# Attention prologue: x loaded first, the stacks cleared in halves, and their row blocks moved to partitions 0-23 and 64-87

## What is computed

```python
q, k, v = split(x @ wq + bq), split(c @ wk + bk), split(c @ wv + bv)
scores = einsum("bhqd,bhkd->bhqk", q, k) * scale
o = einsum("bhqk,bhkd->bhqd", softmax(scores), v)
x + merge(o) @ wo + bo
```

## Time and profile before

| | |
|---|---|
| runs | 5312.48 us median of 3 (5310.64 to 5335.13) |
| profiled execution | 5331.78 us |
| its span, first to last instruction | 5330.1 us |
| X: SP's first load, first scores | 2517.45, 2568.38 us |
| F: the same | 3087.01, 3145.86 us |
| N: the same | 4058.88, 4105.02 us |
| Y: the same | 4643.76, 4689.13 us |

### The profile page before, as it was taken

The page is one execution under the profiler, slowest core; times in us unless marked ns, Lnnn a source line. Parts: engine busy times, 40 slices in busy tenths (PEclk is TensorE's granted clock), DMA queues, the critical chain, the costliest instruction groups (busy, mean ns, idle before and its releaser), DMA issues. The chain is left out here.

```text
span 5330.1 us, 104454 instructions
## 1 busy us (share of the span) xinstructions
PE 4007.7 (75%) x29689; PEld 2312.2 (43%) x29692; DVE 4292.2 (81%) x8421; ACT 2778.3 (52%) x6469; POOL 3235.8 (61%) x3458
## 2 busy tenths in 40 slices
PE   5887888778788887785789958886292888779953
PEld 2333333333333333332466635665282666556632
DVE  5999999999999999996688867775145788767778
ACT  4555555555555555553577724444373455444535
POOL 6888878888888887885677733333544222333345
PEclk8999898998998998988899969996695899889975
DMA  2101111111011111110566546665115555466621
GB/s 85 68 34 70 70 70 38 68 70 70 38 66 70 70 56 50 70 68 14 95 107 111 88 81 111 108 114 157 50 53 118 100 105 105 74 120 113 116 57 32
DMA packets 320191, 420.69 MB, mean 79 GB/s; under 512 B 40000, under 2 KB 301712, under 8 KB 309136
## 3 DMA queue, kind: packets, MB, share of 16 engines
q1 hardware_dynamic: 315536, 408.35, 33.1%
q0 software_dynamic: 4352, 8.95, 0.5%
HBM read 307.65 MB, written 109.58 MB: 78 GB/s over the span
## 5 line engine op out<-in xcount | busy, mean ns | idle before, releaser
L2205 POOL TENSOR_TENSOR m_h<-m_dtu,m_Bb 128x512 f32<-128x512 f32 x1024 | 1595.7, 1588 | 152.6 <-PE bank L1838 150.1
L1838 PE MATMUL bank<-m_h,ident 128*128 128x512 f32 x2048 | 1237.7, 695 | 411.4 <-DVE m_h L2104 405.0
L1838 PEld LDWEIGHTS bank<-m_h,ident 128*128 128x128 f32 x2048 | 368.4, 209 | 1088.9 <-DVE m_h L2104 937.1
L2098 DVE TENSOR_TENSOR_SCAN m_h<-m_dA,m_h 128x512 f32<-128x512 f32 x512 | 773.5, 1511 | 0.5
L2104 DVE TENSOR_TENSOR m_h<-m_h,bank 128x512 f32<-128x512 f32 x1024 | 673.1, 657 | 12.7 <-PE bank L1831 12.7
L2098 DVE TENSOR_TENSOR_SCAN m_h<-bank,m_h 128x512 f32<-128x512 f32 x512 | 620.8, 1212 | 16.7 <-ACT bank L1986 9.5
L1986 ACT ACTIVATE m_dA<-m_dt,m_A 128x512 f32<-128x512 f32 x512 | 366.9, 717 | 356.5 <-DVE m_h L2098 350.1
L1986 ACT ACTIVATE bank<-m_dt,m_A 128x512 f32<-128x512 f32 x512 | 352.5, 688 | 379.3 <-DVE m_h L2098 273.7
L691 DVE TENSOR_REDUCE x_nm<-bank 128x4 f32<-128x308 f32 x512 | 242.4, 474 | 166.6 <-PE bank L364 163.7
L535 ACT ACTIVATE x_sm<-bank,x_nm 128x77 f32<-128x77 f32 x1024 | 318.2, 336 | 62.2 <-DVE x_nm L691 61.8
L691 DVE TENSOR_REDUCE f_nm<-bank 128x4 f32<-128x512 f32 x256 | 175.9, 688 | 111.6 <-PE bank L364 110.9
(11 more groups left out here) (424 smaller groups left out, 10364.4 us busy)
## 6 DMA issues: line engine op xcount, KB each, us to landing
m_Bb<-m_B SPq DMA_DIRECT2D x32, 4096.0 KB, 12.1
x_Ks<-x_k_parts SPq DMA_DIRECT2D x32, 462.0 KB
x_q_parts<-x_qp SPq DMA_DIRECT2D x32, 384.0 KB, 4.2
x_Qs<-x_q_parts SPq DMA_DIRECT2D x32, 384.0 KB
f_Ks<-f_k_parts SPq DMA_DIRECT2D x16, 768.0 KB
a_Ks<-a_k_parts SPq DMA_DIRECT2D x16, 768.0 KB
x_xp<-x_stage SPq DMA_DIRECT2D x32, 256.0 KB
x_Qs<-x_q_parts SPq DMA_DIRECT2D x32, 256.0 KB
```

The lines of the kernel that those rows point to most:

```text
L1838: pe.matmul(banks[4 + c], ident[:], h[:, k % RING, :], start=(s == 0), stop=(s == NS - 1)).then_inc(s_ya.sem, 1)
L2098: v.tensor_tensor_scan(h[:, k % RING, :], decays[k % AHEAD], h[:, k % RING, :], 0.0, ALU.mult, ALU.add).then_inc(s_h.sem, 1)
L2205: pool.tensor_tensor(h[:, k % RING, :], dtu[:, d, c, :], Bb[:, d, s, :], ALU.mult).then_inc(s_dB.sem, 1)
```

## The change

SP loads x of the first group before the weights, and in F the weights of the LayerNorm ahead of the others. The waits for all weights move: on TensorE and ScalarE behind the turning and copying of the first x, on VectorE in front of the first group's values (in F of its norm), on GpSimd they are gone. Each stack is cleared in halves, one per group: Ks by VectorE at its start and behind the first group's preparation, Qs by ScalarE in the same places, as an `activation` that copies a constant times 0 over a half as fp32. nmT and pT are cleared by VectorE behind the first group's preparation. The second halves have a semaphore of their own, on which SP waits before the second group's fill. The six blocks move from partitions 0-47 to 0-23 and 64-87 (Q: 24 rows at 0, 16 at 64, 8 at 80), and Ks is filled by two transfers of 24 rows.

```diff
-    PARTS, ROWS = 3, 6 * DH
+    PARTS = 3
     K_TIMES = (3, 2, 1)
+    Q_ROWS = (0, 8 * DH, 10 * DH)
+    K_ROWS = ((0, 0, 3), (8 * DH, 3, 6))
+    FILLS = len(Q_ROWS) + len(K_ROWS)
...
+        zeros = half_pow[:, 0:1].unsqueeze(1).to_broadcast([P, H, GT // 2])
...
             def fill_stack(g, par):
+                if isinstance(g, int) and g == 1:
+                    sp.wait_ge(s_zero1.sem, 2)
...
-                at = 0
-                for parts in K_TIMES:
-                    fill(Qs[at * DH:(at + parts) * DH, par], dram_q[par, 0:parts])
-                    at += parts
-                fill(Ks[0:ROWS, par], dram_k[par])
+                for row, parts in zip(Q_ROWS, K_TIMES):
+                    fill(Qs[row:row + parts * DH, par], dram_q[par, 0:parts])
+                for row, lo, hi in K_ROWS:
+                    fill(Ks[row:row + (hi - lo) * DH, par], dram_k[par, lo:hi])
...
             load_x(0, 0)
+            load_weights()
             load_x(1, 1)
...
         def _(pe):
-            pe.wait_ge(s_w.sem, 16 * NW)
...
                     if g == 0 or slot[u] < 0:
                         prep(u, g, g)
+                    if g == 0 and u == "x":
+                        pe.wait_ge(s_w.sem, 16 * NW)
...
-            act.wait_ge(s_w.sem, 16 * NW)
-            if rms or bq is not None:
+            def clear_queries(par, zeroed):
+                act.activation(Qs[:, par].bitcast(F32), zeros, ACT.Copy, scale=0.0).then_inc(zeroed, 1)
...
+            clear_queries(0, s_zero.sem)
             for g in range(2):
                 for u in uses:
...
                     if u != "v" and (g == 0 or slot[u] < 0):
                         prep(u, g, g)
+                    if g == 0 and u == "x":
+                        scale_bias()
+                if g == 0:
+                    clear_queries(1, s_zero1.sem)
...
-            dve.memset(Ks[:], 0.0).then_inc(s_zero.sem, 1)
-            if gate is None:
-                dve.memset(nmT[:], 0.0).then_inc(s_zero.sem, 1)
-            if sk < P:
-                dve.memset(pT[:], 0.0).then_inc(s_zero.sem, 1)
-            dve.wait_ge(s_w.sem, 16 * NW)
-            dve.wait_ge(s_setup.sem, 1)
+            dve.memset(Ks[:, 0], 0.0).then_inc(s_zero.sem, 1)
...
                         if g == 0 or z < 0:
+                            if g == 0 and f is (front_norm if ln is not None else value_rows):
+                                v.wait_ge(s_w.sem, 16 * NW)
                             f(v, ch, g, g)
+                    if g == 0:
+                        if gate is None:
+                            v.memset(nmT[:], 0.0).then_inc(s_zero.sem, 1)
+                        if sk < P:
+                            v.memset(pT[:], 0.0).then_inc(s_zero.sem, 1)
+                        v.memset(Ks[:, 1], 0.0).then_inc(s_zero1.sem, 1)
...
         def _(pool):
-            pool.wait_ge(s_w.sem, 16 * NW)
-            pool.sem_inc(s_step, 1)
...
-            pool.memset(Qs[:], 0.0).then_inc(s_zero.sem, 1)
```

More of the change, by code:

```diff
@@ L166, in attention @@
         lvar = sb("lvar", [P, 2, GB]) if ln is not None else None
-        s_w = sem("weights"); s_setup = sem("setup"); s_zero = sem("zeroed"); s_xp = sem("x_loaded"); s_xr = [sem(f"residual_loaded{l}", 16) for l in range(2)]
+        s_w = sem("weights"); s_setup = sem("setup"); s_zero = sem("zeroed"); s_zero1 = sem("second_stacks_zeroed"); s_xp = sem("x_loaded"); s_xr = [sem(f"residual_loaded{l}", 16) for l in range(2)]
         s_xpfree = sem("x_used"); s_pb = sem("proj_written", NU); s_pf = sem("proj_evacuated", NU)
@@ L171, in attention @@
         s_mid = sem("mid_ready", 2); s_lo = sem("lo_ready", 2)
-        s_ps = sem("parts_stored", 16 * (PARTS + 1)); s_stk = [sem(f"stack_loaded{l}", 16 * (PARTS + 1)) for l in range(2)]
+        s_ps = sem("parts_stored", 16 * (PARTS + 1)); s_stk = [sem(f"stack_loaded{l}", 16 * FILLS) for l in range(2)]
         s_ln = sem("front_var", 1); s_lp = sem("front_pow", 1); s_xn = sem("front_norm", 1)
@@ L210, in _, with load_weights @@
         def _(sp):
-            n = 0
             def load_w(dst, src):
                 sp.dma_start(dst, src).then_inc(s_w.sem, 16)
[L214 to L228, removed]
+            def load_weights():
+                if ln is not None:
+                    for j, t in enumerate(ln):
+                        load_w(lnw[:, j, :], t.rearrange("(a d) -> a d", a=1).to_broadcast([P, D]))
+                for j, t in enumerate((wq, wk, wv, wo)):
+                    load_w(w[:, j, :], t)
+                for j, t in enumerate((bq, bk)):
+                    if t is not None:
+                        load_w(bqk[:, j:j + 1], t.rearrange("(d a) -> d a", a=1))
+                if rms:
+                    for j, t in enumerate(rms):
+                        load_w(bqk[:, j:j + 1], t)
+                if bv is not None:
+                    load_w(bvb[:], bv.rearrange("(a d) -> a d", a=1).to_broadcast([P, D]))
+                if bo is not None:
+                    load_w(bob[:], bo.rearrange("(a d) -> a d", a=1).to_broadcast([P, D]))
             def load_x(g, par):
@@ L480, in _, with scale_bias @@
         def _(act):
-            act.wait_ge(s_w.sem, 16 * NW)
-            if rms or bq is not None:
-                act.activation(bqk[:, 0:1], bqk[:, 0:1], ACT.Copy, scale=scale).then_inc(s_bq.sem, 1)
-                act.wait_ge(s_bq.sem, 1)
+            def clear_queries(par, zeroed):
+                act.activation(Qs[:, par].bitcast(F32), zeros, ACT.Copy, scale=0.0).then_inc(zeroed, 1)
+            def scale_bias():
+                act.wait_ge(s_w.sem, 16 * NW)
+                if rms or bq is not None:
+                    act.activation(bqk[:, 0:1], bqk[:, 0:1], ACT.Copy, scale=scale).then_inc(s_bq.sem, 1)
+                    act.wait_ge(s_bq.sem, 1)
             def evac(g, u, dst, src, **k):
@@ L576, in _ @@
                     if rms and u == "qn":
+                        if g == 0:
+                            act.wait_ge(s_setup.sem, 1)
                         root(g)
```

## The result

The changed kernel takes 5272.1 us (median of 5 runs, 5259.4 to 5279.7) against 5322.9 us for the kernel before on the same chip (5 runs, 5310.6 to 5335.1): a ratio of 0.9902, 95% interval 0.9885 to 0.9919. It is 1% faster, inside the range and of the sign forecast. 43 us were forecast, 51 came. That the forecast in us (5269) lies nearer than that is luck: the three runs it started from were low, 5312.5, where the five sessions of this study have medians of 5319.0 to 5327.4 for the kernel before.

The account below looks back on a forecast made before the run. TensorE's idle time before the first scores of four attention stages, mainly behind GpSimd's clearing, was the target: 11.4 + 15.9 + 1.6 + 10.4 + 4 = 43 us off the 5312.48 us median gave 5269 us, range 5237 to 5300.

Parts of the forecast that it names:

- X, F, Y: Prologues of gated cross attention, attention with LayerNorm in front, plain cross attention: 11.4, 15.9 and 10.4 us won.
- The mechanism of the clearing: In X, GpSimd's 13.75 us clearing of Qs holds VectorE's first q cast at 9.79 us instead of 0.43.
- N: Prologue of the attention with RMS norms: x copied out earlier, after ScalarE's clearing, 1.6 us won (0.5 to 2.8).
- The fill: Stack fills before the first scores, in the new partition layout: 1 us less each, 4 us over four stages.
- My count of rows per engine (8 against 7): Fills: the busiest DMA engines carry 8 rows instead of 7, 1.7 us more per fill at the same pace.
- Rival (a): Fills run at the first microsecond's pace: 12 us more come off, 55 in all, 5257 us; chance 0.14.
- (b): Fills get longer by 2.5 us, also delaying Y's loop: 20 us won, 5292 us; chance 0.11 with its like.
- (c): K's two transfers on twelve engines bound Y's loop: at 6 us longer fills 47 us lost, 5359; chance 0.06.
- "Groups in the loops as long as before": Attention loops after the prologues: a sign of being right was that their groups take as long as before.
- Rival (d): Prologues: the clearing was not what held VectorE, so only about 14 us is won, 5298 us; chance 0.03.

Follow-up runs that it names:

- e5: Kernel before, with GpSimd's clearing of the Q stacks cut into 32 instructions instead of one; ratio to before 1.0001.
- e2: Changed kernel with the six blocks back in partitions 0-47 and K filled by two transfers of 24 rows; ratio to before 0.9957.
- e1: Changed kernel with the six blocks back in partitions 0-47 and K filled by one transfer; ratio to before 0.9942.
- e3: Changed kernel with the six blocks in partitions 40-87 and K filled by one transfer of 48 rows; ratio to before 0.9886.
- e6: Kernel before, with the Q stacks cleared by ScalarE ahead of its wait for the weights, not by GpSimd; ratio to before 0.9961.
- e7: Kernel before, with only the order of loads and the waits for weights as in the change, GpSimd still clearing; ratio to before 0.9991.
- e10: Changed kernel with the six blocks in every second partition from 16 to 110 and K filled by one transfer; ratio to before 0.9870.

## Why the prediction was right, and where not

**X, F, Y: right.** 11.4 us forecast for SP's second load, 11.35 measured; 15.9 for F's norm, 16.6 measured (24.29 us after the first load before, 7.71 after, since all weights landed sooner than I put them); 10.4 for Y's fill, 10.75 measured, with pT's clearing as the step that releases it, as said.

**The mechanism of the clearing: half right.** "The clearing holds VectorE, and all the splitting waits" failed as an explanation in e5: without the hold the splitting still waits, in GpSimd's queue. The rows had it: in the earlier trace rows the clearing ends at 2541.21, and the operation after the cast belongs to the engine that clears. The sum came out because the change moves the clearing off that queue.

**N: mis-sized.** 1.6 us forecast; x is copied out 2.96 us sooner and the fill starts 2.1 us sooner. I let ScalarE's clearing start with VectorE's, 1.8 us after the stage's first load; it starts with that load. At 3.62 us (3.7 taken) it ends 0.6 us before the copy and costs nothing.

**The fill: right in sum, by errors that cancel.** 1 us each forecast, 4 in all. From the last transfer's issue to the first scores it is 2.1, 1.2, 1.9 and 1.1 us less, 6 in all; but five transfers take 0.4 us longer to issue than four, which I named (0.35 us) and which has no term in the sum. From the first issue, where the other terms end, 1.7, 0.6, 1.5 and 0.7 us are won, 4.4 in all. My count of rows per engine (8 against 7) costs 0.5 to 1.1 us by e2 against e1 and the change against e3, and not 1.7; the placement, for which no row of before stood, gives 1.9 to 3.0. That this term came so near is luck. Rival (a)'s 4 us each was too much, (b) and (c) had the wrong sign.

**"Groups in the loops as long as before": wrong.** The layout's shorter fills leave fewer of TensorE's long stalls. Mean over the six profiles with old rows and the seven with new ones: F's loop 493.7 and 487.0 us, N's 522.4 and 512.7, stalls in the two together 17 and 5 us. That is 16 us that my sum had at nothing, 12 of them stalls; in the profile of the changed kernel alone F gave 10 and Y's own stalls took 5 back. The clock has a part in it: N's loop ran at 1.2 GHz for 89 us on average with old rows and for 78 with new ones (F's 75 and 73), which at half speed I estimate at up to 6 us. That the stalls are late instructions is what the packets of q8 point to; it was not tried by itself.

**Rival (d)** falls with e6: 28.6 us for the clearing alone.

## What to carry to other kernels

When an instruction on one engine is long because another engine's is running, look first at whose instruction comes next in the chain: if it stands in the second engine's own queue, freeing the first wins nothing, and the setup work has to leave that queue. Put a transfer's rows in partitions both below and above 64, where the consumer doesn't care which rows it contracts; spacing them out shortened the fills further, though not the whole clearly. And price a transfer that overlaps a loop by the loop's stalls too, not only by who waits for its data.

## What was not expected of the hardware

A clearing of 128x16384 bf16 on GpSimd held a cast and a tensor_scalar on VectorE, but not VectorE's own clearing: in e7 pT's clearing runs beside it in the 3.47 us that it takes alone.

```profile
2511.19 13.75 POOL L831 MEMSET x_Qs<- 128x16384 bf16 x1 [0.15 <-POOL x_hide L826]
...
2514.67 3.47 DVE L602 MEMSET x_pT<- 128x4096 f32 x1 [0.80 <-issue]
...
2520.46 4.76 DVE L656 CAST x_qp<-x_qf 128x512 bf16<-128x512 f32 x1 [2.32 <-ACT x_qf L491]
```

The same 1.5 MB into the same tiles by the same four transfers took 14.5, 11.4 or 9.7 us in F by the choice of partitions alone (e1, e3, e10). And with a fill in flight or just over, TensorE stood still for 1.4 to 6.9 us at a time in the loops of F and N, in front of matmuls that wait for no semaphore, until the fills were left out.
